# Attention kernel: an earlier layer norm in step 6, some high parts made by the activation engine, one tile in another place

## What is computed

```python
x = x + 0.5 * ffn(layernorm(x), w1, b1, w2, b2)   # ffn: gelu(x @ w1 + b1) @ w2 + b2, hidden width 1024
x = x + attn(layernorm(x), w_qkv, w_out, b_out)
x = x + 0.5 * ffn(layernorm(x), w1, b1, w2, b2)
# attn: softmax(q k^T / 8 - slope[h] * |i - j|, causal) @ v, heads joined, @ w_out + b_out
```

## Time and profile before

| | us |
|---|---|
| median of three runs | 2273.06 (2267.17 to 2273.5) |
| the profiled execution | 2274.33 |
| its span, first to last instruction | 2272.1 |
| PE busy | 2169.4 (95%) |
| DVE busy | 1549.6 (68%) |
| ACT busy | 1200.7 (53%) |
| POOL busy | 1049.2 (46%) |
| mean granted clock of PE | 0.985 |

### The profile page before, as it was taken

How to read it: one execution, slowest core, us unless ns; L and a number is a source line. 1 busy time by engine, 2 the same in 40 slices (tenths; PEclk the granted TensorE clock), 3 DMA queues, 4 the chain that set the end, 5 groups by cost and what they waited for, 6 DMA issues and landing times.

```text
span 2272.1 us, 41791 instructions
## 1 busy us (share of the span) xinstructions
PE 2169.4 (95%) x14720; PEld 1754.7 (77%) x14720; DVE 1549.6 (68%) x4070; ACT 1200.7 (53%) x3032; POOL 1049.2 (46%) x1770
## 2 busy tenths in 40 slices
PE   6899999999999999999999999999999999999977
PEld 5688787877878778787887878778787787877856
DVE  6776767667676676767667676676766667766653
ACT  4645646365463654736456463654636447364552
POOL 1643627345362553716436273453635437264360
PEclk9999999999999999999999999999999999999988
DMA  3422505134051331504225051340514315042150
GB/s 125 121 76 66 137 4 157 49 89 117 21 148 38 109 97 41 141 24 134 72 67 137 3 155 51 89 117 18 146 42 112 94 34 148 25 128 77 51 144 11
DMA packets 109936, 193.90 MB, mean 85 GB/s; under 512 B 34464, under 2 KB 53152, under 8 KB 109728
## 3 DMA queue, kind: packets, MB, share of 16 engines
q1 hardware_dynamic: 89248, 138.77, 21.6%
q0 software_dynamic: 20480, 52.47, 9.3%
HBM read 14.95 MB, written 8.39 MB: 10 GB/s over the span
## 4 chain that ended last, share of the span: by engine, by line
PE 71%; DVE 15%; ACT 8%; POOL 3%; issue 2%; SPq 1%; DMA 1%; DVEq 0%; POOLq 0%; ACTq 0%
PE ps L269 69%; DVE P L711 4%; DVE gl L636 4%; ACT P L548 4%; DVE gh L682 3%; POOL P L859 3%; PE ps L323 2%; DVE P L703 1%; ACT L548 1%; ACT L533 1%; SPq L219 1%; DVE xtl L636 1%; ACT gt L533 1%; ACT xth L525 0%; ACT qk L515 0%
## 5 line engine op out<-in xcount | busy, mean ns | idle before, releaser
L859 POOL TENSOR_SCALAR P<-P,rs 128x512 f32<-128x512 f32 (+3 forms) x1024 | 535.3, 540 | 453.1 <-DVE rs L694 447.9
L548 ACT ACTIVATE P<-P,mx 128x512 f32<-128x512 f32 (+3 forms) x1024 | 562.0, 552 | 172.2 <-DVE mx L703 171.9
L219 POOL DMA_DIRECT2D PT<-P x640 | 321.6, 508 | 295.2 <-DVE P L711 281.1
L711 DVE STREAM_TRANSPOSE P<-P 128x1792 f32<-128x1792 f32 (+1 forms) x256 | 372.5, 1484 | 12.2 <-POOL P L859 11.6
L269 PE MATMUL ps<-PT,v 128*64 128x256 f32 (+1 forms) x3072 | 309.4, 351 | 32.0 <-DMA PT<-P 32.0
L269 PE MATMUL ps<-w2h,gh 128*128 128x256 f32 x1024 | 305.7, 299 | 28.9 <-DVE gl L636 24.0
L269 PE MATMUL ps<-qk 64*128 64x512 f32 (+3 forms) x2048 | 313.1, 445 | 6.7 <-ACT qk L515 6.7
L269 PEld LDWEIGHTS ps<-PT,v 128*64 128x64 f32 x3072 | 207.8, 138 | 127.9 <-issue 41.7
L515 ACT ACTIVATE qk<-ps 128x512 f32<-128x512 f32 x256 | 153.0, 598 | 270.6 <-PE ps L269 270.6
L269 PE MATMUL ps<-w2l,gh 128*128 128x256 f32 x1024 | 294.3, 287 | 0.0
L269 PE MATMUL ps<-w2h,gl 128*128 128x256 f32 x1024 | 293.8, 287 | 0.0
(11 more groups left out here) (74 smaller groups left out, 4408.0 us busy)
## 6 DMA issues: line engine op xcount, KB each, us to landing
PT<-P SPq DMA_DIRECT2D x1408, 80.0 KB, 2.6
PT<-P POOLq DMA_DIRECT2D x640, 80.0 KB, 2.7
x<-in_L_attn_x SPq DMA_DIRECT2D x16, 512.0 KB, 4.2
out_y<-x SPq DMA_DIRECT2D x16, 512.0 KB, 3.2
raw<-in_L_ffn_w SPq DMA_DIRECT2D x2, 512.0 KB, 5.8
raw<-in_L_ffn_w SPq DMA_DIRECT2D x1, 1024.0 KB, 8.7
rawq<-in_L_attn_w_qkv SPq DMA_DIRECT2D x1, 1024.0 KB, 6.7
rawk<-in_L_attn_w_qkv SPq DMA_DIRECT2D x1, 1024.0 KB, 8.7
```

The costliest lines, as they stand in the source:

```text
L219: e.dma_start(PT[c % 2][32 * m:32 * m + 32, g, :], P[c % 3][32 * g:32 * g + 32, m, :]).then_inc(landed[c % 3].sem, 16)
L548: e.activation(p, p, ACT.Exp, bias=mx[:, r, i:i + 1], scale=-1.0, accum_out=sm[:, r, i:i + 1]).then_inc(s_ex.sem, 1)
L711: e.transpose(p, p).then_inc(s_tr.sem, 1)
L859: e.tensor_scalar(p, p, rs[:, 2 * (c % 2) + h, i:i + 1], 1.0, ALU.mult, ALU.mult).then_inc(s_nz.sem, 1)
```

## The change

It has six parts.

1. In step 6 PE transposes the two units of xn ahead of `values(b, 4)` and not behind it. ACT's `ln_hi` and DVE's `ln_lo` move with them, from the start of step 7 to the end of step 6, and so does `inverse(b, 6, 0)`.
2. In step 7 DVE turns the first half of pair 6 ahead of `biased(b, 7, 3)`.
3. For odd m of the first feed-forward (blocks 1 to 15) ACT makes gh by an ACTIVATE Copy right behind gelu m, and DVE's CAST of it goes.
4. Tile 5 of gh and gl lies where xn lay (XN); tiles 6 and 7 lie in P0, and PT0 isn't used. ACT does gelu 5 ahead of `out_copy(b, 6)`.
5. The second v projection of block b+1 goes between the two units of the third layer norm, on bank 4 (from the list 4, 5); ACT's copy moves with it. Unit 1 then takes the bank of unit 0.
6. Banks: up 0 and 1 take 6 and 7, up 2 bank 0.

```diff
--- before.py
+++ after.py
@@ -53,6 +53,7 @@
     sm = place("sm", [128, 4, NT], F32)
     rs = place("rs", [128, 4, NT], F32)
     xb = [place(f"x{i}", [128, NT, D], F32) for i in range(2)]
+    XN = at[0]
     xn = place("xn", [128, NT, D], F32)
     xth, xtl = place("xth", [128, NK, T], F32R), place("xtl", [128, NK, T], F32R)
     at_o = at[0]
@@ -66,7 +67,7 @@
     PT = [place(f"PT{i}", [128, 4, GW], F32, PT_AT + 16 * GW * i) for i in range(2)]
     gt = [place(f"gt{i}", [128, T], F32, a) for i, a in enumerate((GT, GT + 2048, PP + 28672))]
 
-    g_at = {1: [QK, QK + 4096, V, PP + 20480, PP + 24576, PP, PP + 4096, PT_AT],
+    g_at = {1: [QK, QK + 4096, V, PP + 20480, PP + 24576, XN, PP, PP + 4096],
             2: [at_o + 4096 * m for m in range(4)] + [PP + 20480, PP + 24576, PT_AT + 10240, PT_AT + 14336]}
     gh = {f: [place(f"gh{f}{m}", [128, T], F32R, a) for m, a in enumerate(g_at[f])] for f in (1, 2)}
     gl = {f: [place(f"gl{f}{m}", [128, T], F32R, a + 2048) for m, a in enumerate(g_at[f])] for f in (1, 2)}
@@ -160,8 +161,10 @@
     s_rc = Signal("rc_done", per_half)
     s_tr = Signal("turned_in_place", per_half)
     s_ll = Signal("ll_done", units)
-    s_gh = Signal("gh_done", hidden)
+    s_gh = Signal("gh_done", [k for k in hidden if not (k[0] == 1 and k[1] > 0 and k[2] % 2)])
     s_gs = Signal("gs_done", hidden)
+    by_act = [(1, b, m) for b in B if b > 0 for m in range(1, NM, 2)]
+    s_ga = Signal("gh_by_act", by_act)
     s_ol = Signal("ol_done", outs)
     s_r1 = Signal("r1_done", [(f, b, t) for f, b, t in down if f == 1])
     s_r3 = Signal("r3_done", [(f, b, t) for f, b, t in down if f == 2])
@@ -435,13 +438,17 @@
                     for tile in v_tiles(c):
                         proj_tile(b, tile)
                     if more and c == NC - 1:
-                        among[0] = (0, 1, 6, 7)
-                        up(1, b + 1, range(3))
-                    values(b, c - 2)
+                        up(1, b + 1, range(2))
+                        among[0] = (0, 1)
+                        up(1, b + 1, [2])
                     if more and c == NC - 2:
                         ln_transpose(1, b + 1, 0)
                         among[0] = (5,)
                         ln_transpose(1, b + 1, 1)
+                        among[0] = (6, 7)
+                    values(b, c - 2)
+                    if more and c == NC - 2:
+                        turn[0] = 5
                 if more:
                     among[0] = (2, 3, 4, 5)
                     up(1, b + 1, range(3, 6))
@@ -480,10 +487,14 @@
                     ln_transpose(2, b + 1, 1)
                 out_proj(b, 3)
                 if b + 1 < NB:
-                    for tile in tiles[:FIRST]:
+                    for tile in tiles[:FIRST - 1]:
                         proj_tile(b + 1, tile)
                 among[0] = (6, 7)
                 ln_transpose(3, b, 0)
+                if b + 1 < NB:
+                    among[0] = (4, 5)
+                    proj_tile(b + 1, tiles[FIRST - 1])
+                    among[0] = (6, 7)
                 ln_transpose(3, b, 1)
                 among[0] = range(8)
                 if b + 1 < NB:
@@ -532,6 +543,9 @@
                         e.wait_ge(s_gs.sem, s_gs.at(hidden[n0 + m - 3]))
                     e.activation(gt[m % 3][:, :], bank_of(("up", f, b, m)), ACT.Gelu,
                                  bias=b1c[:, m:m + 1]).then_inc(s_gl.sem, 1)
+                    if (f, b, m) in s_ga.value:
+                        e.wait_ge(s_gl.sem, s_gl.at((f, b, m)))
+                        e.activation(gh[f][m][:, :], gt[m % 3][:, :], ACT.Copy).then_inc(s_ga.sem, 1)
 
             def out_hi(b, t):
                 if t == 0:
@@ -565,9 +579,6 @@
                 proj_copy(b, ("q", 2))
                 exps(b, 1, 1)
                 for c in range(2, NC):
-                    if more and c == NC - 1:
-                        ln_hi(1, b + 1, 0)
-                        ln_hi(1, b + 1, 1)
                     if c >= 3:
                         out_copy(b, c - 3)
                     exps(b, c, 3)
@@ -581,14 +592,17 @@
                     for tile in v_tiles(c)[1:]:
                         proj_copy(b, tile)
                     exps(b, c, 1)
+                    if more and c == NC - 2:
+                        ln_hi(1, b + 1, 0)
+                        ln_hi(1, b + 1, 1)
                 if more:
                     gelu(1, b + 1, range(2))
                 out_copy(b, NC - 3)
                 if more:
-                    gelu(1, b + 1, range(2, 5))
+                    gelu(1, b + 1, range(2, 6))
                 out_copy(b, NC - 2)
                 if more:
-                    gelu(1, b + 1, range(5, NM))
+                    gelu(1, b + 1, range(6, NM))
                 out_copy(b, NC - 1)
 
             def split_hi(key, dst, src, scale):
@@ -623,9 +637,11 @@
                 if b + 1 < NB:
                     ln_hi(2, b + 1, 0)
                     ln_hi(2, b + 1, 1)
-                    for tile in tiles[:FIRST]:
+                    for tile in tiles[:FIRST - 1]:
                         proj_copy(b + 1, tile)
                 ln_hi(3, b, 0)
+                if b + 1 < NB:
+                    proj_copy(b + 1, tiles[FIRST - 1])
                 ln_hi(3, b, 1)
                 gelu(2, b, range(NM))
 
@@ -678,9 +694,12 @@
 
             def gelu_split(f, b, ms):
                 for m in ms:
-                    e.wait_ge(s_gl.sem, s_gl.at((f, b, m)))
-                    e.tensor_copy(gh[f][m][:, :], gt[m % 3][:, :]).then_inc(s_gh.sem, 1)
-                    e.wait_ge(s_gh.sem, s_gh.at((f, b, m)))
+                    if (f, b, m) in s_ga.value:
+                        e.wait_ge(s_ga.sem, s_ga.at((f, b, m)))
+                    else:
+                        e.wait_ge(s_gl.sem, s_gl.at((f, b, m)))
+                        e.tensor_copy(gh[f][m][:, :], gt[m % 3][:, :]).then_inc(s_gh.sem, 1)
+                        e.wait_ge(s_gh.sem, s_gh.at((f, b, m)))
                     residue(gl[f][m][:, :], gt[m % 3][:, :], gh[f][m][:, :]).then_inc(s_gs.sem, 1)
 
             def out_lo(b, t):
@@ -740,14 +759,12 @@
                 begin(b)
                 for c in range(2, NC):
                     if more and c == NC - 1:
-                        inverse(b, c - 1, 0)
-                        ln_lo(1, b + 1, 0)
-                        ln_lo(1, b + 1, 1)
+                        turned(b, c - 1, 1)
                         biased(b, c, 3)
                     else:
                         biased(b, c, 3)
                         inverse(b, c - 1, 0)
-                    turned(b, c - 1, 1)
+                        turned(b, c - 1, 1)
                     turned(b, c - 1, 0)
                     biased(b, c, 2)
                     biased(b, c, 0)
@@ -761,6 +778,10 @@
                     if more and c == 5:
                         for t in range(NT):
                             normal(1, b + 1, t)
+                    if more and c == 6:
+                        inverse(b, c, 0)
+                        ln_lo(1, b + 1, 0)
+                        ln_lo(1, b + 1, 1)
                 inverse(b, NC - 1, 0)
                 if more:
                     gelu_split(1, b + 1, [0])
```

## The result

| | before | changed |
|---|---|---|
| median | 2272.93 us | 2217.07 us (2216.28 to 2218.28) |
| ratio | | 0.976, 95% interval 0.9743 to 0.9777 |
| span of the profiled execution | 2272.1 us | 2216.5 us |
| from P times V of pair 6 to that of the next block, where nothing else disturbs it | 136.8 us | 134.05 us |
| CAST 0 held for 4.21 us | 4 of 15 blocks | none of 15 |

The forecast was 2225.5 (2207 to 2250). In the lines of the changed kernel matmuls are L272, transposes L326, `residue` L652, CASTs L701, gelus L544 and ACT's new Copies L548.

A forecast was written before the change was run, and what follows sets the result against it. PE, 95% busy, waits for transfers of P (32.0 us) and gl (24.0). Savings 11 x 2.6 + 4 x 2.5 + 15 x 0.2 + 6 = 47.6 from 2274.33, median 1.3 lower: 2225.5 (2207 to 2250).

The forecast's parts named there:

- Parts 1 and 2: Steps 6 and 7: DVE's chain comes 1.3 us sooner, so PE's 1.18 wait for pair 6's transfers goes.
- nothing else in its chain has to be later: DVE's chain into pair 6's transfers: with xtl 1.3 us sooner, no other instruction there is delayed.
- Parts 3 and 4: Down projection: fewer CASTs, gl 1 held 1.8; tile 7 starts 2.6 us sooner a block, transfer wait included.
- the two pieces only change places: PE's step 6: scores of step 7 start from 949.5 in both orders, so no gain there.
- Part 5: Third layer norm: v projection between its units cuts unit 1's wait; 0.2 us a block, bounds 0 and 0.34.
- The held CASTs: CAST 0 on DVE: still held in four of 15 blocks, each such block gaining 2.5 us.
- The clock: Six stretches at 1.2 GHz behind waits in the down projection, 1.5 us each; four go, saving 6 us.
- Part 6 has each bank free 1 us or more ahead of its new user: Bank assignment: every bank is free at least 1 us early, so no new wait.
- Rival (a): gl 1 isn't held and PE no longer stops: gain 62 to 70 us, 2203 to 2211; chance 0.18.
- Rival (b): ACT becomes the bound, its copies taking 0.7 or more: gain 26 us, 2247; chance 0.18.
- (c): Pair 6's transfers start no sooner as DVE's large turn waits for POOL: 2266 to 2268; chance 0.05.
- (d): Slower: CAST 0 held in every block, 30 low-clock stretches, 22 us lost, 2295; chance 0.04.

The follow-up runs named there:

- e11: e1 with DVE's large turn of pair 6 again behind the two wide instructions on the scores of pair 7; 2255.24 us, ratio 0.9927.
- e4: Changed kernel with POOL's bias addition for the next block moved from step 7 into idle time of step 6; 2204.73 us, ratio 0.9688.
- e6: Changed kernel with tile 5 again in P0, tile 7 in PT0, gelu 5 behind the copy of pair 6 to o; 2211.14 us, ratio 0.9733.
- e3: Changed kernel with the second v projection again ahead of both units of the third layer norm; 2217.98 us, ratio 0.9747.
- e9: Changed kernel with the high part of tile 0 made by ACT too; 2251.73 us, ratio 0.9883.
- e1: Changed kernel keeping the new order of steps 6 and 7, without ACT's Copies, tile 5's new place and the v move; 2246.39 us, ratio 0.9871.
- e12: Kernel before with an unread one-column Copy on ACT ahead of gelu 0 in each block; 2270.81 us, ratio 0.9989.
- e2: Changed kernel with the old order of steps 6 and 7 and of the v projection; 2251.93 us, ratio 0.9881.
- e5: Changed kernel with P times V of pair 4 in block 0 put on bank 7; 2214.83 us, ratio 0.9722.
- e8: Changed kernel with the edits of both e4 and e5; 2202.73 us, ratio 0.967.
- e10: Changed kernel with the edits of both e9 and e4; 2205.33 us, ratio 0.9705.
- e7: Kernel before with only POOL's bias addition moved to step 6; 2242.15 us, ratio 0.9844.

## Why the prediction was right, and where it was off

The spans differ by 55.6 us; forecast were 47.6. The mechanism was right in its main terms; two small terms were mis-sized, both to the same side.

- **Parts 1 and 2: right.** Small turn to P times V 9.02 for 9.06, wait of 1.18 gone, xth straight behind the last exponential. What the text didn't see is that "nothing else in its chain has to be later" holds by part 2 alone (e11).
- **Parts 3 and 4: right in mechanism, the size in part by luck.** gl 1 took 1.82 for 1.8. An ordinary block is 2.75 shorter in all; forecast were 2.6 + 0.2. But tile 7 starts 8.46 after P times V, where the working had 971.1 - 962.9 = 8.2, so the down projection gave 1.2 and not 1.46. Two things fill the gap: the wait for the transfers gave 1.27 from start to start for its bracket of 1.18, and step 6 gave 0.15, which the working put at nothing ("the two pieces only change places"): from its last projections to the scores of step 7 PE took 6.31 before and takes 6.15. e4 shows that the hold of gl 1 is the cause of the rest. Inside this term part 4 has the other sign than its place in the change suggests (e6); the working had the 0.5 of the copy to o in it, and took it as given.
- **Part 5: right** in size, 0.23 for 0.2, though part of it is given back (e3).
- **The held CASTs: mis-sized.** "I keep four in 15" was the step that failed. There was none, which is 4 x 2.3 = 9 us more. The reason given, that both sides of the race "move together by 1.3", is true to 0.01 us (2.47 both times) and not to a nanosecond: CAST 0 now comes some 10 ns earlier against POOL, and all its holds that were seen lie in a band narrower than that (last section).
- **The clock: mis-sized.** All six stretches went and not four, 3 us more. The working left half of the four in blocks with a held CAST, and these blocks were gone. Kernels in which PE still stopped several times in the down projection had some (before 6, e9 7, e1 4, e12 4, e2 2, e11 1); those in which it hardly did had none (changed, e3, e4, e5, e6, e8, e10), nor had e7.
- **Block 0: a wrong sentence.** "Part 6 has each bank free 1 us or more ahead of its new user" was worked out for a middle block. In block 0 banks 6 and 7 are swapped, and PE waits 2.06 there (e5), 2 us less gained.

Together: 15 x 2.75 + 4 x 2.3 + 6 x 1.5 - 2 = 41 + 9 + 9 - 2 = 57, against 55.6. Read from the blocks, the 15 are 58.9 shorter in sum, and P times V of pair 6 in block 0 comes 2.9 later than before (140.16 for 137.24), of which the bank explains 2.06.

Rival (a), gl 1 not held, is out by the 1.82. Rival (b), ACT as the bound, is out since its copies take 0.63 and not 0.7, DVE waits for a gh of ACT only once, 0.2 us, and the waits of PE went when the bias was moved and ACT's work was left as it was (e4). (c) is out since the wait of 1.18 is gone, (d) since no CAST was held.

## What to carry to other kernels

When an engine's work collides with another engine's instructions, and it has idle time elsewhere, the idle time is the place for it: one line that moved POOL's addition by a step was worth more than half of the whole rewrite, and on top of it another 12 us. Where an instruction is moved off an engine because it is held, look at what comes to stand in its place; the next one was held nearly as long (3.87 for 4.21 in e9). Read a race between two engines in nanoseconds before you call it unchanged. Work out the first block by itself when a bank or a buffer is given out in turn.

## What was not expected of the hardware

DVE instructions that come while POOL runs its eight multiplications back to back are at times held far longer than one POOL instruction. In the kernel before CAST 0 comes 2.47 after POOL's start both where it gets in (0.79, block 6) and where it is held (4.21, block 4). POOL shows it from the other side. In block 6 its eight multiplications take 4.85, in block 4 they run undisturbed:

```profile
681.10 4.08 POOL L859 TENSOR_SCALAR P<-P,rs 128x512 f32<-128x512 f32 x8
685.15 2.34 POOL L854 TENSOR_TENSOR x<-x,b2h 128x1024 f32<-128x1024 f32 x1
```

So where DVE gets in, POOL's sixth and seventh multiplication wait for it (0.60 and 1.00 us for 0.36 and 0.47), and where it doesn't, it waits for all that POOL has left, the bias included. gl 0 of block 6 fits in: it comes 3.29 after POOL's start, the sixth multiplication ends at 3.41, and its 0.85 is 0.16 over the 0.69 alone. The prediction read this row as no full block; it can as well be a full block of what was left of one short instruction.

The views round to 0.01 us, the traces have nanoseconds. POOL's fifth multiplication starts near 2.46, and against that start CAST 0 comes, in the nine kernels that have the CAST and the bias behind the multiplications:

| kernel | CAST 0 behind the start of POOL's fifth multiplication, ns | held for over 4 us |
|---|---|---|
| e11 | -9 to -3 | none of 15 |
| changed | -7 to 2 | none |
| e5 | -6 to 1 | none |
| e6 | -7 to 3 | 1, the one at 3 |
| before | 8 to 15 | 4, all at 9 |
| e2 | 9 to 16 | 7, at 9 and 10 |
| e1 | 14 to 23 | none |
| e3 | 14 to 25 | none |
| e12 | 69 to 81 | none |

All 12 holds lie between 3 and 10 ns, and so do 11 CASTs that were let in; of the 112 outside none was held. Other instructions fit in: gl 0, where it follows a CAST 0, comes 0.1 or more away from any start on POOL and took 0.84 or 0.85 in each of 168 blocks, while in e9, where it was held in 15 of 15, it comes 32 to 40 ns ahead of the start of the seventh multiplication. So a long hold was only seen for an arrival at the change from one POOL instruction to the next. What decides there isn't shown: no run set the distance, POOL's times are the roughest of the profile, and in e4 11 CASTs came 5 to 9 ns behind the start and none was held. When a hold ends is open too: with the bias behind the multiplications it lasted until the bias was done, without it it ended ahead of the last multiplication (1.48 in e7, 1.06 in e10).

The spread of times goes with it in part. Before ranged from 2262.9 to 2287.1 in its 18 runs on one chip, and e2 over 14.6 us, while kernels whose profiles had no held instruction or one in every block stayed within 2 to 6 us (changed, e1, e3, e4, e5, e8 to e11). e6, with one hold, had 4.2; e7, with its holds of 1.48, had 7.1, and e12 had 12 without a held CAST in its one profile. Only one execution of each kernel was profiled, so that the holds make the spread isn't shown.
